# Token sums on DVE in the attention, a scalars store one quad later in the queue, and the second pass's block loads placed ahead of stores and scalars

## What is computed

```python
x = x + tanh(g_xattn) * attention(layernorm(x), k = [ctx, xn @ wk.T], v = [ctx, xn @ wv.T])   # 8 batches, 512 keys, one head
x = x + tanh(g_ffn) * ffn(layernorm(x))

# ffn, for the N = 2048 tokens
scores = softmax(x @ gate_w.T)                      # 64 experts
w_e = the 8 largest of them, the others 0
scalar = w_e by group of 8, summed                  # 8 groups
soft = softmax(where(w_e == 0, -1e9, w_e)) in each group
xg = x + soft @ mask_up_w                           # per group
a = silu(xg @ gate_proj.T) * (xg @ up_proj.T)       # 352 inner rows per group
y = sum over groups of scalar * (a @ down_proj.T)
```

## Time and profile before

| | |
|---|---|
| median of 3 runs | 1096.89 us |
| profiled execution, its own time | 1099.27 us |
| its span, first to last instruction | 1097.5 us |
| granted TensorE clock over the span | 0.989 |
| PE busy | 1056.5 us (96%) |
| PE's weight loads busy | 895.8 us (82%) |
| DVE busy | 746.9 us (68%) |
| POOL busy | 634.1 us (58%) |
| ACT busy | 379.8 us (35%) |
| chain that ended last | PE 76%, DVE 12%, DMA 3%, issue 3%, SP's queue 2%, ACT 2%, POOL 1% |

### The profile page before, as it was taken

The page is one execution under the profiler, slowest core; times in us unless marked ns, Lnnn a source line. Parts: engine busy times, 40 slices in busy tenths (PEclk is TensorE's granted clock), DMA queues, the critical chain, the costliest instruction groups (busy, mean ns, idle before and its releaser), DMA issues.

```text
span 1097.5 us, 14456 instructions
## 1 busy us (share of the span) xinstructions
PE 1056.5 (96%) x5388; PEld 895.8 (82%) x5388; DVE 746.9 (68%) x1320; ACT 379.8 (35%) x635; POOL 634.1 (58%) x511
## 2 busy tenths in 40 slices
PE   7999999999999869999999999999999999999998
PEld 7889988988887657888877788878888888888886
DVE  7775665766667845878788988746656655665665
ACT  4333323433323333334244333323233333323331
POOL 0212203533515826866888888756777776677761
PEclk8999999999999998999999999999999999999999
DMA  9112225356685252023332633294322112212202
GB/s 333 61 40 96 60 47 145 65 157 164 176 249 176 77 54 73 28 81 46 92 104 60 125 110 121 80 324 137 105 73 72 43 57 73 72 47 71 72 27 77
DMA packets 114134, 111.64 MB, mean 102 GB/s; under 512 B 20881, under 2 KB 96401, under 8 KB 114065
## 3 DMA queue, kind: packets, MB, share of 16 engines
q1 hardware_dynamic: 113696, 110.58, 35.2%
q10 hardware_dynamic: 368, 0.15, 0.1%
HBM read 79.05 MB, written 31.65 MB: 101 GB/s over the span
## 4 chain that ended last, share of the span: by engine, by line
PE 76%; DVE 12%; DMA 3%; issue 3%; SPq 2%; ACT 2%; POOL 1%; DVEq 0%; ACTq 0%
PE bank L76 40%; PE bank L1605 29%; PE bank L1611 3%; PE bank L1438 1%; DVE a_stack L1288 1%; DVE tmp L1297 1%; DMA wgu_raw<-in_w_gate_up 1%; PE bank L1619 1%; SPq L460 1%; DVE tmp L1413 1%; DVE xres L1304 1%; DMA x2t<-token_sums_l 1%; DVE tmp L1401 1%; DVE a_stack L1286 1%; DVE soft L1137 1%
## 5 line engine op out<-in xcount | busy, mean ns | idle before, releaser
L1605 PE MATMUL bank<-x2t,wgu_hi 128*128 128x512 f32 x1144 | 354.2, 391 | 0.0
L649 POOL TENSOR_TENSOR wgu_lo<-wgu_raw,wgu_hi 128x512 fp32r<-128x512 f32 (+1 forms) x129 | 210.4, 1637 | 97.5 <-ACT wgu_hi L796 95.8
L1605 PEld LDWEIGHTS bank<-x2t,wgu_hi 128*128 128x128 f32 x1144 | 215.7, 189 | 44.4
L1605 PE MATMUL bank<-x2t,wgu_lo 128*128 128x512 f32 x572 | 225.6, 394 | 5.6 <-DMA x2t<-token_sums_l 2.7
L796 ACT CAST wgu_hi<-wgu_raw 128x512 fp32r<-128x512 f32 (+1 forms) x129 | 93.7, 727 | 231.4 <-PE bank L1611 188.9
L1304 DVE TENSOR_TENSOR xres<-xres,bank 128x512 f32<-128x512 f32 x176 | 120.0, 682 | 54.6 <-PE bank L76 54.5
L1605 PEld LDWEIGHTS bank<-x2t,wgu_lo 128*128 128x128 f32 x572 | 107.9, 189 | 30.6 <-issue 4.9
L76 PE MATMUL bank<-wd_hi,at_second 128*128 128x512 f32 x336 | 130.8, 389 | 0.0
L76 PE MATMUL bank<-wd_hi,at_first 128*128 128x512 f32 x256 | 99.9, 390 | 2.4 <-issue 2.4
L1297 DVE TENSOR_TENSOR tmp<-tmp,scalars 128x512 f32<-128x512 f32 x88 | 99.1, 1127 | 3.0
L1348 DVE TENSOR_TENSOR tmp<-tmp,bank 128x512 f32<-128x512 f32 x44 | 30.2, 686 | 94.8 <-PE bank L1605 94.2
(11 more groups left out here) (213 smaller groups left out, 2253.5 us busy)
## 6 DMA issues: line engine op xcount, KB each, us to landing
wgu_raw<-in_w_gate_up SPq DMA_DIRECT2D x43, 512.0 KB, 4.2
wd_raw<-in_w_down SPq DMA_DIRECT2D x22, 512.0 KB, 4.9
a_stacks<-a_stack SPq DMA_DIRECT2D x22, 192.0 KB, 1.9
a_stack<-a_stacks SPq DMA_DIRECT2D x22, 192.0 KB, 4.0
ctxt_raw<-in_ctx_t SPq DMA_DIRECT2D x8, 512.0 KB, 11.7
ctx_raw<-in_ctx SPq DMA_DIRECT2D x8, 512.0 KB, 9.4
x<-x_raw SPq DMA_DIRECT2D x8, 512.0 KB, 4.0
sums_raw<-x SPq DMA_DIRECT2D x16, 256.0 KB, 3.9
```

The lines of the kernel that those rows point to most:

```text
L649: nc.gpsimd.tensor_tensor(wgu_lo[:, group], raw_of(quad)[:, group], f32(wgu_hi[:, group]), ALU.subtract).then_inc(s_fw_lo, 1)
L1605: last = nc.tensor.matmul(out_bank[:], stationary, moving, start=begins and n == 0, stop=n == len(pairs) - 1, skip_group_check=True)
```

## The change

Four things are changed.

First, the four subtractions that form a piece's sums move from POOL to DVE for the pieces 0 to 3, in batches 5 and 6. The first piece of a batch is formed behind `qt_lo`, the second behind `v_lo`. ACT rounds the first where it rounded both, and the second only after the exponentials and `we_t`; POOL takes both low parts at the end of its batch, behind the context's low parts.

Second, `store_scalars(B - 3)` moves in SP's list from quad 2 to quad 3, where it stands behind the loads of that quad.

Third, at quad 21 the block loads 1 and 2 of the second pass go ahead of the store of the masked stack, and the blocks 3 to 6 ahead of the scalars' four transfers. A new semaphore, on product 5, lets block 4 wait for the product that reads its place.

Fourth, at quad 2, ACT copies the first down weights ahead of its first silu, and POOL forms their low part ahead of the second group of the next quad's weights.

```diff
--- before.py
+++ after.py
@@ -364,6 +364,7 @@
         s_a, s_a_masked, s_a_diff, s_a_hi, s_a_st = map(sem, ("a_ready", "a_masked", "a_diff", "a_hi", "a_stack_done"))
         s_a_out = [sem(f"a_stored{j}") for j in range(2)]
         s_a_in = [sem(f"a_loaded{j}") for j in range(2)]
+        s_p5 = sem("product5_read")
         s_m1, s_m6, s_m2, s_m5, s_c11, s_m7, s_m4, s_m3 = map(
             sem, ("m1_ready", "m6_ready", "m2_ready", "m5_ready", "c11_ready", "m7_ready", "m4_ready", "m3_ready"))
         s_s1, s_s2, s_s3, s_c22, s_c21, s_c12 = map(
@@ -552,6 +553,7 @@
                     store_x2(B - 2, x2r_hi, x2r_lo)
                 if q == 2:
                     store_x2(B - 1, x2r_hi, x2r_lo)
+                if q == 3:
                     store_scalars(B - 3)
                 if q == 8:
                     store_soft(B - 3)
@@ -562,6 +564,10 @@
                     store_scalars(B - 1)
                 if q == 19:
                     store_soft(B - 1)
+                if q == 21:
+                    for order, read in enumerate((s_m1, s_m6)):
+                        sp.wait_ge(read, q + 1)
+                        load_block(1, order + 1)
                 if quad.first_pass:
                     sp.wait_ge(s_a_st, q + 1)
                     sp.dma_start(a_dram[q], f32(a_stack[:, j]).rearrange("p m r -> p (m r)")).then_inc(s_a_out[j], 16)
@@ -580,14 +586,11 @@
                 if q == 21:
                     sp.wait_ge(s_m3, q)
                     load_soft(1, 0)
-                    for order, read in enumerate((s_m1, s_m6, s_m2)):
+                    for order, read in enumerate((s_m2, s_p5, s_m7, s_m4)):
                         sp.wait_ge(read, q + 1)
-                        load_block(1, order + 1)
+                        load_block(1, order + 3)
                     sp.wait_ge(s_act, 2 * q)
                     load_scalars(1, 0)
-                    for order, read in enumerate((s_m5, s_m7, s_m4)):
-                        sp.wait_ge(read, q + 1)
-                        load_block(1, order + 4)
                 if q == 22:
                     load_soft(1, 1)
                     sp.wait_ge(s_act, 2 * q)
@@ -673,17 +676,15 @@
                                         ALU.subtract).then_inc(s_piece_lo, 1)
 
             for b in range(2, B):
-                pieces = (2 * (b - 5), 2 * (b - 5) + 1) if b in (5, 6) else ()
-                for i in pieces:
-                    piece_sums(i)
-                for i in pieces:
-                    piece_low(i)
                 if b == B - 1:
                     weight_sums(quads[0])
                     for n, group in enumerate((GROUP_A, GROUP_B, GROUP_C)):
                         weight_low(quads[0], n, group)
                 x2_whole(b - 2, ot_hi, ot_lo)
                 context_lo(b)
+                if b in (5, 6):
+                    for i in (2 * (b - 5), 2 * (b - 5) + 1):
+                        piece_low(i)
 
             def group_a(quad):
                 return GROUP_A if quad.first_pass else GROUP_A_LATER
@@ -714,12 +715,12 @@
                 if q + 1 < QUADS:
                     after = quads[q + 1]
                     weight_low(after, 0, group_a(after))
+                    if q == 2:
+                        for j in range(2):
+                            wd_low(0, j)
                     weight_low(after, 1, GROUP_B)
                     if q == 0:
                         x2_whole(B - 2, x2r_hi, x2r_lo)
-                    if q == 2:
-                        for j in range(2):
-                            wd_low(0, j)
                     if 3 <= q < QUADS - 2:
                         weight_sums(quads[q + 2])
                     weight_low(after, 2, GROUP_C)
@@ -812,7 +813,6 @@
 
                 if b in (5, 6):
                     piece_high(2 * (b - 5))
-                    piece_high(2 * (b - 5) + 1)
                 if not part.next:
                     for n, group in enumerate((GROUP_A, GROUP_B, GROUP_C)):
                         weight_high(quads[0], n, group)
@@ -853,6 +853,8 @@
                         norm_hi(1)
                 if part.route:
                     weights_copy(r)
+                if b in (5, 6):
+                    piece_high(2 * (b - 5) + 1)
                 if part.next and not part.first:
                     norm_hi(b + 1)
                 if part.stack:
@@ -971,6 +973,8 @@
                     late_x2_hi(B - 2, 4)
                     eng.wait_ge(s_m7, q + 1)
                     weight_high(after, 1, GROUP_B)
+                if q == 2:
+                    down_weights(0)
                 eng.wait_ge(s_c11, q + 1)
                 if q >= 2:
                     eng.wait_ge(s_at_lo, 2 * q - 3)
@@ -984,8 +988,6 @@
                     eng.wait_ge(s_x2_out, 32 * (B - 1))
                     eng.wait_ge(s_x2_raw, B - 1)
                     late_x2_hi(B - 1, 6)
-                if q == 2:
-                    down_weights(0)
                 if q == QUADS - 1:
                     down_weights(UNITS - 1)
                 if after:
@@ -1171,11 +1173,31 @@
                 dve.wait_ge(s_rinv, b + 1)
                 nc.vector.tensor_scalar(out_coef[:], row_inv[:], gain[:, 0:1], None, ALU.mult).then_inc(s_coef, 1)
 
+            def piece_sums(i):
+
+                raw = sums_raw[piece_home(i)]
+                chunk_0, chunk_1 = raw[:, 0], raw[:, 1]
+                low, high = slice(0, 2), slice(2, 4)
+                dve.wait_ge(s_piece_in[piece_home(i)], 32 * (i // 2 + 1 if i < PIECES else i - PIECES + 1))
+                nc.vector.tensor_tensor(chunk_0[:, low], chunk_1[:, low], chunk_0[:, low],
+                                        ALU.subtract).then_inc(s_piece_sum, 1)
+                dve.wait_ge(s_piece_sum, 4 * i + 1)
+                nc.vector.tensor_tensor(chunk_1[:, low], chunk_1[:, high], chunk_1[:, low],
+                                        ALU.subtract).then_inc(s_piece_sum, 1)
+                dve.wait_ge(s_piece_sum, 4 * i + 2)
+                nc.vector.tensor_tensor(chunk_1[:, high], chunk_1[:, high], chunk_0[:, low],
+                                        ALU.subtract).then_inc(s_piece_sum, 1)
+                dve.wait_ge(s_piece_sum, 4 * i + 3)
+                nc.vector.tensor_tensor(chunk_0[:, high], chunk_0[:, high], chunk_1[:, high],
+                                        ALU.subtract).then_inc(s_piece_sum, 1)
+
             def iteration(b, part):
                 r = b - 2
                 for j in range(2):
                     at = slice(2 * j, 2 * j + 2)
                     lo_of(s_q_hi, s_q_lo, 2 * b + j + 1, qt_lo[:, at, :], bank[j][:], qt_hi[:, at, :])
+                if b in (5, 6):
+                    piece_sums(2 * (b - 5))
                 def key_lo(j):
                     at = slice(2 * j, 2 * j + 2)
                     lo_of(s_k_hi, s_k_lo, 2 * b + j + 1, kt_lo[:, at, S:KEYS], bank[2 + j][:], kt_hi[:, at, S:KEYS])
@@ -1202,6 +1224,8 @@
                 if part.first:
                     for j in range(2):
                         weight_lo(3, j)
+                if b in (5, 6):
+                    piece_sums(2 * (b - 5) + 1)
                 if part.route:
                     route_top(r)
                 for t in range(ST):
@@ -1678,7 +1702,7 @@
                 q, psum_c = quad.q, banks_of(quad)[2]
                 if quad.first_pass:
                     pe.wait_ge(s_a_masked, q + 1)
-                product(psum_c, W_S1, quad, 3, True)
+                product(psum_c, W_S1, quad, 3, True).then_inc(s_p5, 1)
 
             def product_7(quad):
                 q, psum_b = quad.q, banks_of(quad)[1]
```

## The result

The changed kernel took 1084.3 us in the median of four runs (1082.05 to 1085.04), the kernel before 1096.85 (1095.05 to 1097.58). The ratio is 0.9885, 95% interval 0.9866 to 0.9903, so 12.6 us faster; the forecast was 1080.2, its range 1075 to 1089. The profiled execution took 1084.04 us (span 1082.2, granted clock 0.995).

What follows compares the result with a forecast made beforehand. PE was taken as busy nearly throughout, so only its gaps and slow stretches could be gained. Terms -13.0 - 4.6 - 1.0 + 1.4 - 1.5 + 2.0 = -16.7 us gave a forecast median of 1080.2, range 1075 to 1089.

Steps and rivals of the forecast that it cites:

- Quad 4: Scalars' store behind quad 3's loads ends POOL's weight wait and the slow clock: 30.56 to 17.6 us, 13.0 gained.
- Quad 22: Earlier block loads of the second pass remove PE's wait and slow clock: 20.50 to 15.94 us, 4.6 gained.
- Quad 2: Earlier first down weights let DVE's first add of a down tile come sooner: 1.0 us gained, bounds 0 and 2.4.
- Batch 5: DVE's token sums delay the keys and `ot_lo`, so PE waits 1.4 us at the logits: +1.4 us.
- where on POOL they were not DVE's concern: Held-sums rival: the 16 subtractions contend with POOL only once on DVE; its case above 1099 us had chance 0.06.
- Batch 6: Should look like batch 5, 41.6 us for 43.10, if its pieces are loaded in time: -1.5 us.
- The lateness kept as risk: In batch 6, pieces could load late for DVE's sums: 1 us kept as risk.
- Batch 7: First weights go 3.0 us after its start, PE waits some 2.4 at the logits: +2.0 us.
- parts lost: Rival: quad 2, second pass, batch 7's clock and batch 6's load lose gains; 1082.5 to 1089 us, chance 0.18.
- the second slow stretch of batch 7: Within the lost-gains rival, batch 7's slow clock comes twice: +1.6 us; that rival's chance 0.18.
- The jam: Rival: quad 6's weights land late behind the scalars' store, stalling PE in quad 5; 1089 to 1099 us, chance 0.07.
- count of nine held ones: Subtractions on DVE held by POOL, 2.0 us each; from nine on, the case above 1099 us, chance 0.06.

Runs made afterwards that it cites:

- the second edit alone: The kernel before with only the scalars' store moved from quad 2 to quad 3 in SP's list: 1084.85 us, ratio 0.9874.
- the third: The kernel before with only the second pass's block loads put ahead of stores and scalars: 1093.76 us, ratio 0.9958.
- The fourth edit alone: The kernel before with only the first down weights taken earlier on ACT and POOL: 1099.83 us, ratio 1.0017.
- `route_groups` moved away: The changed kernel with DVE's four `route_groups` operations in quad 2 behind its first three down-tile adds: 1081.5 us, ratio 0.9856.
- The early rounding: The changed kernel with ACT rounding the second piece's sums ahead of the exponentials in batches 5 and 6: 1081.57 us, ratio 0.9864.
- half the bundle: The kernel before with only the scalars' store moved and the second pass's block loads earlier in SP's queue: 1080.04 us, ratio 0.9837.
- the run with the down weights back: The changed kernel with ACT and POOL taking the first down weights where they did before: 1084.63 us, ratio 0.9889.

## Why the prediction was right, and where not

- **The direction and most of the size** rest on SP's order, as predicted: the second edit alone gives 13.8 us (11.7 in the rest of its profile) and the third 4.6, by the chain of the earlier trace rows and the block of the earlier trace rows.
- **Quad 4**, -13.0 forecast, -12.2 measured. The mechanism was right, the 17.6 us taken from quad 10 was off. Quad 4 takes 18.33 to 18.39 in every kernel with the edit. DVE is busier there than in quad 10 (15.9 us against 14.1 in the earlier trace rows), and in the changed kernel's trace PE has waits of 0.3 and 0.2 us for it, and is busy 17.90 us for 17.63.
- **Quad 22** was right to 0.1 us, and its slow clock went with the gap as assumed.
- **Quad 2 is the step that failed.** The prediction said: "So the add can come at 378.36 and ends at 379.05", and took 1.0 us of gain, "since POOL's moved operation can hold DVE". It read DVE's 0.60 us of idleness as slack and gave the hold 0.1 us. The hold was 1.9 us on the first two operations on `soft`. The slack took up 0.6 of it, and the scaling ahead of the add, 1.64 us before and 1.09 now, another 0.55, so the add came 0.7 us later instead of 0.6 earlier. The wait was only passed from `wd_lo` to DVE. The fourth edit alone shows the loss, and with `route_groups` moved away quad 2 gains 1.6 us. Most of the +1.9 is not the wait but the slow clock behind it (1.6), and that part is in some measure chance: quad 2 also had a slow stretch, 18.55 and 18.60 us, in two kernels without the edit. Without the clock the step is still wrong, +0.35 for -1.0.
- **Batch 5**, +1.4 forecast, +0.5 measured. Subtractions, rounding and keys were sized rightly, but DVE's queries came 0.9 us earlier than assumed (`qt_lo` starts 6.1 us after the batch's start, 7.0 before), so PE waited 0.3 us at the logits and not 1.4. With POOL's sums gone two of DVE's small operations at the batch's start fell from 0.64 and 0.59 us to 0.17 each. The short ones are in all seven kernels here with the sums on DVE; the seven with the sums on POOL have two of 0.4 to 0.6 us there, and `qt_lo` at 6.8 to 7.0. The prediction's "where on POOL they were not DVE's concern" was wrong, and the move had a gain that it missed.
- **Batch 6** was right to 0.1 us, in part by luck. The lateness kept as risk came, since DVE waits 0.85 us for the third piece, and the queries' gain made up for it (`qt_lo` starts 6.1 us after the start here too).
- **Batch 7**, +2.0 forecast, +2.5 measured. The first weights went 4.3 us after the start and not 3.0. The store of the last low part took 6.2 us for 4.7. PE waited 3.6 us at the logits for the 2.4 forecast, but the wait of 2.0 at the stack, forecast to shrink by 0.4, went altogether; that makes 1.6, and the rest is a longer slow stretch (0.92 for 0.96). The nearness of the sum is luck. Against the batch without a slow clock (40.4 to 40.9 us) the price is nearer 4. The early rounding shows that the late second rounding is the cause: with it the batch takes 39.25.
- **The cases.** The time fell into "parts lost". Of its parts quad 2 came, and worse than at zero gain; the second slow stretch of batch 7 came in part (0.9 us of 1.6 in PE's busy time), and so did the late load in batch 6. The jam did not move, and POOL held none of the 16 subtractions: those in the changed kernel's trace took 0.41 to 0.43 us. The prediction's count of nine held ones is one short: nine cost 18 us, 1098.2, and only ten pass 1099.

## What to carry to other kernels

In an engine that issues transfers in order, ask of each wait what stands behind it: one store moved behind the loads gave about all that the change gave. When work is moved between engines that hold each other, price the operations that already stand at the new place and at the old one, not only the moved ones; DVE's operations on `soft` lost 1.9 us in one place, and its small ones won 0.9 in the other. Make each part of a bundled change alone: here two of four cost time, and half the bundle was 4 us faster than all of it. Where single effects are of 1 to 3 us and slow stretches of the clock come and go, compare stages over many profiles and not one pair.

## What the runs showed of the hardware

Operations with one SBUF input were held beside POOL too: `soft<-flat`, a TENSOR_SCALAR over 128 elements, took 0.22 us in quad 2 before, 1.15 in quad 2 after and in batch 6 of the changed kernel 2.04, ending as POOL's operation did:

```profile
244.96 2.04 DVE L1138 TENSOR_SCALAR soft<-flat 128x128 f32<-128x128 f32 x1
...
244.53 2.39 POOL L631 TENSOR_TENSOR x_raw<-ot_hi,ot_lo 128x1024 f32<-128x1024 f32 x1 [16.13 <-DVE ot_lo L1051]
```

The same stage comes with and without a stretch at 1.2 GHz in different runs: batch 7, with the sums on POOL, takes 40.85 us at 1.00 and 42.14 at 0.96, quad 2 17.02 at 1.00 and 18.60 at 0.91, with the same wait of 2.4 us in the latter pair. In the run with the down weights back the slow stretch came ahead of a wait, which shrank from 2.4 to 0.8 us, and quad 2 took 17.06 us at 0.90 where it takes 17.02 and 17.05 at 1.00. The start-up up to the end of batch 0 varies in the same way: 40.59 us at 1.00 in the changed kernel, 43.24 at 0.92 in the kernel before. What decides whether the clock falls behind such a wait stays open.
